# Six of eight sequences routed inside attention, experts begun on part of their tokens

## What is computed

```python
h = layernorm(x) * (1 + ca) + sa
x = x + ga * attention(h)          # layer 0: causal, 16 heads of 16, one shared K and V head, rotary
h = layernorm(x) * (1 + cb) + sb
x = x + gb * experts(h)            # layer 0
# experts: logits = h @ Wg + bg; probs = softmax over the 512 tokens of a sequence, per expert
#          vals, idx = top_k(probs, 64) for each of 8 sequences x 16 experts
#          tok = h[idx]; three 256x256 layers (relu, relu, none); times vals; added back at idx
# layer 1: the same frame, linear attention, then a coupling network of three cycles
```

## Time and profile before

| | us |
|---|---|
| median of 3 runs | 1191.42 (1188.3 to 1193.76) |
| the profiled execution | 1191.18 |
| its span in the trace | 1189.4 |
| PE busy | 1070.3 (90%) |
| DVE, ACT, POOL busy | 733.1, 596.0, 465.7 |
| last logits evicted by ACT | 478.17 |
| tables of the routing done | 503.21 |
| first gather issued, last scatter issued | 507.23, 712.21 |
| first PE work of the linear attention | 722.03 |

### The profile page before, as it was taken

One profiled execution on the slowest core, in us unless ns is written; L12 is line 12 of the kernel. 1 busy time (PEld: TensorE's weight loads), 2 busy tenths in 40 slices (PEclk: granted clock), 3 DMA queues, 4 the chain that ended last, 5 costly groups with the idle time before them and its releaser, 6 DMA issues. The chain is left out here.

```text
span 1189.4 us, 19798 instructions
## 1 busy us (share of the span) xinstructions
PE 1070.3 (90%) x6630; PEld 603.6 (51%) x6630; DVE 733.1 (62%) x1549; ACT 596.0 (50%) x1133; POOL 465.7 (39%) x692
## 2 busy tenths in 40 slices
PE   5499999999999998479999865999999998999996
PEld 3244554454454543346656432556666674455554
DVE  2667878787787783624333323767777781665665
ACT  3167677676766666013333324534444435866732
POOL 2444635444453511068888873333333310000000
PEclk9599999999999999579999987999999998999988
DMA  3522415233241411436676771011211002001001
GB/s 133 112 46 29 82 29 99 63 70 77 57 93 32 73 39 59 150 107 137 165 158 137 178 136 32 6 60 41 77 41 41 19 20 89 1 27 56 25 27 45
DMA packets 73685, 85.31 MB, mean 72 GB/s; under 512 B 12577, under 2 KB 67817, under 8 KB 73457
## 3 DMA queue, kind: packets, MB, share of 16 engines
q1 hardware_dynamic: 61296, 67.27, 21.6%
q0 software_dynamic: 12288, 16.79, 8.2%
HBM read 45.58 MB, written 25.47 MB: 60 GB/s over the span
## 5 line engine op out<-in xcount | busy, mean ns | idle before, releaser
L560 DVE TENSOR_REDUCE nmax<-psum 128x1 f32<-128x512 f32 (+3 forms) x352 | 215.6, 637 | 44.9 <-PE psum L779 39.7
L677 ACT ACTIVATE pT<-psum 128x512 f32<-128x512 f32 x320 | 181.1, 596 | 65.6 <-PE psum L800 35.6
L777 PE MATMUL psum<-k6T,q6T 96*128 96x512 bf16 (+3 forms) x512 | 128.2, 310 | 17.8 <-DVE nmax L560 14.0
L797 PE MATMUL psum<-q6T,k6T 99*128 99x512 bf16 x320 | 119.4, 382 | 1.1 <-ACT pT L677 0.9
L1085 POOL DMA_INDIRECT residual<-expert_y,idx_e x64 | 101.0, 1578 | 22.0 <-issue 16.5
L777 PEld LDWEIGHTS psum<-k6T,q6T 96*128 96x128 bf16 x512 | 45.7, 99 | 91.6 <-DVE nmax L560 59.1
L1604 DVE TENSOR_TENSOR l_scores<-psum,const_sb 128x512 f32<-128x512 f32 x128 | 79.5, 684 | 20.3 <-PE psum L1779 20.3
L779 PE MATMUL psum<-negs_bf,ident_bf 128*128 128x128 bf16 (+2 forms) x352 | 88.8, 252 | 0.0
L812 PE MATMUL psum<-pT,v 128*32 128x512 f32 x640 | 85.0, 604 | 0.0
L1072 POOL DMA_INDIRECT expert_tokens<-router_input,idx_e x64 | 62.7, 980 | 52.4 <-POOLq L903 33.2
L1737 PE MATMUL psum<-l_hT,l_w 128*128 128x512 f32 x128 | 63.7, 621 | 0.8 <-ACT l_plus_one L1681 0.8
(11 more groups left out here) (298 smaller groups left out, 2220.5 us busy)
## 6 DMA issues: line engine op xcount, KB each, us to landing
q6T<-q_parts SPq DMA_DIRECT2D x96, 128.0 KB, 4.5
expert_w<-in_ew SPq DMA_DIRECT2D x16, 768.0 KB, 4.8
x_in<-in_x SPq DMA_DIRECT2D x8, 512.0 KB, 4.3
residual<-x SPq DMA_DIRECT2D x32, 128.0 KB, 1.9
router_input<-h SPq DMA_DIRECT2D x32, 128.0 KB, 1.8
l_x<-residual SPq DMA_DIRECT2D x8, 512.0 KB, 4.3
x_dram<-l_x SPq DMA_DIRECT2D x32, 128.0 KB, 1.7
out<-c_out SPq DMA_DIRECT2D x16, 256.0 KB, 2.1
```

Source lines behind the costliest of these rows:

```text
L560: dve.tensor_reduce(nmax[:, i, u * nh:(u + 1) * nh], ps_s[:, n % SR, 0:nh * (i + 1) * P].rearrange("p (h k) -> p h k", h=nh), AX_X, ALU.ma ...
L677: act.activation(pT[:, n % PR].rearrange("p h t -> p (h t)"), ps_t[:, n % TR, :], ACT.Exp, scale=HD ** -0.5).then_inc(probs, 1)
L777: pe.matmul(out[:, a, :], q6T[0:6 * HD, b % 2, u * nh + a, i * P:(i + 1) * P], k6T[0:6 * HD, b % 2, 0:w], start=a == 0, stop=False, skip_g ...
L797: last = pe.matmul(out, k6T[:, b % 2, j * P:(j + 1) * P], q6T[:, b % 2, hg * 4:hg * 4 + 4, i * P:(i + 1) * P], start=True, stop=j < i)
```

## The change

1. The first sequence's `kv` and `sp` are placed ahead of its second `Q`; only `load_rows(0)` stands before the input of sequence 1, the other two follow the second `qd`; `qd` waits for each part by itself.
2. Logits go straight to SBUF. `lg` of sequence 4 and `h2T` and `lg` of sequence 5 stand earlier in the list (places 910 to 972; they stood at 949, 975, 986, 1007, 1026, 1055). From place 1022 on, every second place is a routing step of sequences 0 to 5 (96 rows): 24 for the rounds, one for the tables (`ti`), one for their transposes (`tt`). Place 1022 follows `("S", 7, 3, 14)`; `tt` stands after `("ST", 7, 3, 0, 1)`.
3. With `lg` of sequence 2, SP loads weights of experts 0 and 1, the second modulation matrix and the biases.
4. The routing block is gone. In the expert block experts 0 to 3 run on tiles 0 to 2, then on tile 3, then the rest on four tiles: 20 units. DVE routes sequences 6 and 7 (32 rows) meanwhile, and ACT evicts both halves in the first four units. PE does the second modulation first. Weights have four slots, in the same memory that later holds buffers of the other phases.

```diff
+EARLY_LOGITS = (910, 925, 937, 950, 962, 972)
+EARLY_ROUTING = (1022, 2)
...
+    for first, later in ((("kv", 0), ("Q", 0, 1)), (("sp", 0, 0), ("kv", 0))):
+        order.remove(first)
+        order.insert(order.index(later), first)
+    b = EARLY_SEQS - 1
+    for at, s in zip(EARLY_LOGITS, [("lg", b - 1)] + [("h2T", b, i) for i in range(NT)] + [("lg", b)]):
+        order.remove(s)
+        order.insert(at, s)
+    for n, s in enumerate([("tk", r, part) for r in range(TOPK // 8) for part in range(3)] + [("ti", 0), ("tt", 0)]):
+        order.insert(EARLY_ROUTING[0] + EARLY_ROUTING[1] * n, s)
...
-                        for b in range(3):
-                            load_rows(b)
+                        load_rows(0)
...
-                        sp.wait_ge(q_lo, 2 * b + half + 1)
                         for place, part in enumerate((0, 0, 0, 1, 1, 2)):
+                            sp.wait_ge((q_hi, q_mid, q_lo)[part], 2 * b + half + 1)
...
+                        if b == 0 and half == 1:
+                            for later in range(1, 3):
+                                load_rows(later)
...
+                    if s == ("lg", 2):
+                        sp.wait_ge(row_fill, 1)
+                        for e in range(2):
+                            sp.dma_start(route.w[:, e].rearrange("p l k c -> p (l k c)"), m.d["ew"][e]).then_inc(route.w_in[e], 16)
+                        sp.dma_start(wmod_l1, m.d["wmod"][:, 1]).then_inc(route.mod_loaded, 16)
+                        sp.dma_start(route.par_e[:, :, 4:7], m.d["eb"]).then_inc(bias_loaded, 16)
...
+                    if s[0] == "tt":
+                        n = EARLY_SEQS * E
+                        pe.wait_ge(tables_ready, 1)
+                        pe.transpose(py[:, 0:n], route.idxf[early_rows].rearrange("p r s -> p (r s)"), ident[0:n, 0:n])
+                        pe.transpose(py[:, P:P + n], route.vals[early_rows].rearrange("p r s -> p (r s)"), ident[0:n, 0:n]).then_inc(y_fill, 1)
...
+UNITS = [(e, (0, 1, 2)) for e in range(EARLY)] + [(e, (3,)) for e in range(EARLY)] + [(e, (0, 1, 2, 3)) for e in range(EARLY, E)]
...
+                first, second, every = (0, 1, 2), (3,), (0, 1, 2, 3)
+                for e in range(EARLY):
+                    gather(e, first)
+                scatter(0, first)
+                scatter(1, first)
+                pool.wait_ge(listed, 1)
+                settle(pool, m.passed)
+                for e in range(EARLY):
+                    gather(e, second)
+                scatter(2, first)
+                gather(EARLY, every)
+                scatter(3, first)
+                for e in range(EARLY):
+                    scatter(e, second)
+                    if e:
+                        gather(e + EARLY, every)
...
+                for r in range(TOPK // 8):
+                    route_round(dve, link, route, late, r, top_ready)
...
+                    if r == 4:
+                        dve.wait_ge(gb_loaded, 16 * B)
+                        gate_outputs(0)
+                gate_outputs(1)
+                dve.wait_ge(exp_ready, 2)
+                route_tables(dve, link, m, late).then_inc(tables, 1)
+                dve.wait_ge(turned, 1)
...
+                gate_outputs(2)
+                copy_tokens(EARLY)
+                gate_outputs(3)
```

More of the change, by code:

```diff
@@ new lines, in route_round @@
+def route_round(dve, link, route, rows, r, top_ready, parts=range(3)):
+    part = slice(8 * r, 8 * r + 8)
+    src = route.left if r else route.logits
+    if 0 in parts:
+        found = dve.max(out=route.top[rows, part], in_=src[rows])
+        if r == TOPK // 8 - 1:
+            found.then_inc(top_ready, 1)
+            dve.wait_ge(top_ready, 1)
+        else:
+            link(found)
+    if 1 in parts:
+        link(dve.max_index(out=route.idx[rows, part], in_max=route.top[rows, part], in_values=src[rows]))
+    if 2 in parts and r < TOPK // 8 - 1:
+        link(dve.match_replace(out=route.left[rows], in_to_replace=route.top[rows, part], in_values=src[rows], imm_value=LOWEST))
@@ new lines, in route_tables, with expert_tables @@
+def route_tables(dve, link, m, rows):
+    route, n = m.route, rows.stop - rows.start
+    seq = m.const[rows, C_SEQ:C_SEQ + 1]
+    link(dve.reciprocal(route.total[rows], route.total[rows]))
+    link(dve.tensor_scalar(route.idxf[rows], route.idx[rows].unsqueeze(1).to_broadcast([n, 2, TOPK]), seq, None, ALU.add))
+    return dve.tensor_scalar(route.vals[rows], route.etop[rows].unsqueeze(1).to_broadcast([n, 2, TOPK]), route.total[rows, 0:1], None,
+                             ALU.mult)
+def expert_tables():
+    number, before, count = {}, [], 0
+    for e, tiles in UNITS:
+        before.append(count)
+        for i in tiles:
+            count += 1
+            number[e, i] = count
+    return number, before
@@ L873, in routing_phase, with expert_phase @@
+def expert_phase(nc, m):
+    TOK, YS, WS = 4, 2, 4
+    number, before = expert_tables()
     with ExitStack() as ctx:
@@ L1038, in expert_phase, with columns @@
         ident = m.const[:, C_IDENT:C_IDENT + P]
+        lead = m.lin
         def par(e, n):
-            return m.par_e[:, e, n:n + 1]
+            return par_e[:, e, n:n + 1]
+        def columns(tiles):
+            return slice(tiles[0] * P, (tiles[-1] + 1) * P)
         with nc.Block() as block:
@@ L1118, in _, with turn @@
             def _(pe):
-                def turn(e, k, tiles=range(4)):
-                    if k == 0 and tiles[0] == 0 and e:
-                        pe.wait_ge(t_act, e)
-                    if k == 1 and e:
-                        pe.wait_ge(t_dve, e)
-                    for i in tiles:
+                def turn(u, k, part):
+                    for i in part:
+                        e, tiles = UNITS[u]
+                        if i == tiles[0] and u:
+                            pe.wait_ge(t_half[k], u)
                         if k == 0:
@@ new lines, in _ @@
+                for u in range(len(UNITS)):
+                    e, tiles = UNITS[u]
+                    at = columns(tiles)
+                    for k in range(KC if u < EARLY else 1):
+                        act.wait_ge(l1_fill, KC * u + k + 1)
+                        if u:
+                            act.wait_ge(l2_fill, KC * u)
+                        act.activation(h1[:, k, at], ps_1[:, k, at], ACT.Relu, bias=par(e, 4)).then_inc(l1_half[k], 1)
+                    if u == 2:
+                        act.wait_ge(top_ready, 1)
+                        act.activation(route.etop[late], route.top[late], ACT.Exp, bias=route.nmax[late, 0:1]).then_inc(exp_ready, 1)
+                    for k in range(KC if u < EARLY else 1):
+                        act.wait_ge(l2_fill, KC * u + k + 1)
+                        if u:
+                            act.wait_ge(l3_fill, before[u])
+                        act.activation(h2[:, k, at], ps_2[:, k, at], ACT.Relu, bias=par(e, 5)).then_inc(l2_half[k], 1)
+                    if u + 1 < len(UNITS):
+                        copy_tokens(u + 1)
+                    for i in tiles:
+                        act.wait_ge(l3_fill, max(number[e, j] for j in tiles if j // 2 == i // 2))
```

465 lines of the change are left out of this document (230 added, 235 removed).

## The result

The changed kernel takes 1193.18 us in the median of 12 runs against 1188.70 of the kernel before (12 runs): ratio 1.0034, 95% interval 1.0020 to 1.0047, so about 4.0 us slower (the medians alone differ by 4.5). Two more series gave 1.0036 (1.0024 to 1.0049) and 1.0034 (1.0018 to 1.0051). I had forecast 1190.7 us, 0.7 less than the profiled execution of before, in a range that holds the result; the size is small, but the sign is wrong.

A forecast was written before the change was run, and what follows sets the result against it. PE was taken to bound mid attention, DVE the exposed routing, POOL's gathers and scatters the experts. Terms -5.0 + 13.5 + 2.6 + 0 - 11.8 = -0.7 against 1191.18 gave 1190.5, as median 1190.7 us; range 1181 to 1200.

The forecast's parts named there:

- start of attention: Attention's start: second sequence's input issued and landed earlier, so score reductions resume sooner; -5.0 us, bounds 3 and 7.
- routing inside attention, clock included: Attention's end: PE waits for DVE's routing rounds and tables, 13.5 us, plus 2.6 us for PE's lowered clock.
- change of block, router to S: Between attention and experts: six logit stores on SP instead of eight, next block starts 0.9 us sooner.
- S: Start of the expert block: predicted at 480.75 us plus the delay from attention's start and the routing inside it.
- S to the end of POOL: Expert phase: from block start to POOL's last scatter, predicted 219.7 us; a change of -10.9 us.
- part 1: Start of attention: fewer row loads ahead of the second sequence's input, reductions resume earlier; gain 5.0 us, bounds 3 and 7.
- Part 4: Expert start: earlier block start and experts on three tiles first, POOL ending the phase; -11.8 us, bounds -6 and -15.
- Part 2: Attention's end: routing six sequences on DVE delays PE 13.5 us (bounds 9 and 15), clock adds 2.6 (0 and 5).
- Part 3: Mid attention: 3.1 MB of loads on SP ahead of the row of maxima stay hidden; 0 us, bounds 0 and 13.
- rival B: Mid attention: the 3.1 MB hold up the row of maxima, below 263 GB/s; 1203.7 us at 124 GB/s; chance 0.12.
- rival C: Expert phase: three-tile units stay near 11.2 us, lists come 8.4 us later, gain only 3.4; 1199 us; chance 0.10.
- Rival A: Attention's end: DVE's routing hides better than counted, half of 16.1 us gone; 1182.6 us; chance 0.25.

The follow-up runs named there:

- the best version: Changed kernel with routing steps three places apart, late lists one unit earlier, modulation matmuls split between attention's end and expert start: 1178.38 us, 0.9907 of the kernel before.

## Why the prediction was wrong

Up to POOL's end the sum can be checked term by term (predicted, and measured from the places in the first table):

| term | predicted | measured |
|---|---|---|
| start of attention | -5.0 | -2.07 |
| routing inside attention, clock included | +16.1 | +16.39 |
| change of block, router to S | -0.9 | +0.44 |
| S to the end of POOL | -10.9 | -8.98 |
| sum | -0.7 | +5.78 |

**The step that failed is part 1**, "Gain 5.0, bounds 3 and 7": 2.07, below its own lower bound, and with 2.9 us the largest row of the 6.5. Part 4 with its change of block missed by 3.3 us inside its bounds; each of the two alone turns the forecast's sign. Three things were in part 1. I took the input's issue at 39.4 us, counting only the row loads; the same diff reorders `kv` and `sp`, which puts three of DVE's gate steps beside GpSimd's wide ones (2.8 us longer together) and lets them begin only 1.4 us earlier, so it was 40.85. I had used the reordering only in its favour; undone by itself it gives about 1 us. The landing took 6.7 us and not 4.5 to 6. And of the 2.6 us that the reductions resume earlier, 2.07 arrive at the outputs. The load mattered as I said: it still holds DVE for 2.98 us.

**Part 2 was right in sum, less so inside.** DVE starts the rounds at 442.33 and ends the tables at 464.58 (I said 465.6 without part 1). In pieces: the lead shrinks step by step where the six steps were moved to, by 1.77 us up to 434.57 (2.07 to 0.30), where I had at most 0.6; the wait adds 12.70 (I took 13.5); the half clock behind it 1.67 (2.6); the last steps 0.25. The 96 rows take the time of 128 (0.69 and 0.68 us a step), which settles that bound. The clock fell as the earlier trace rows suggested, in pieces, and was 0.50 for the six us behind the last wait.

**Part 3 was right**: the 3.1 MB cost nothing, and rival B is out; the lead of 2.07 us is the same 85 us later. But my reason was the wrong one. The time for them doesn't count from the logits, as I took it, but from 11.5 us earlier, where the list reaches the loads. The modulation matrix, issued at 299.86, landed 12.0 us later, at 311.9: 3.1 MB in 13.1 us or 240 GB/s, less than the 263 GB/s under which I let rival B begin. The row of maxima was issued at 314.81, when all had landed. So no run tests what I weighed, the row of maxima behind the weights. But another small load stood right behind them in the same queue, the biases, issued at 300.34:

```profile
par_e<-in_eb SPq DMA_DIRECT2D x1, 24.0 KB, 12.0
```

It landed 12.0 us after its issue, at 312.3, just behind the matrix, where the same load took 3.5 us in the kernel before. The Trainium skill, "DMA: Bandwidth & Descriptors", section "Queues, rings and completion order", says that each DMA engine takes the descriptors of a ring in order; this row agrees. Whether the row of maxima, issued in that time, would have been late was not tested.

**Part 4 was 3.3 us too good.** The lists came at S + 42.0, as worked out, and so did the units (8.5 us from the first scatter group to the second; 8.4 predicted), so rival C is out. The 2.6 us for the first unit's half clock were more than their rows gave (5.88 - 3.60 = 2.3, for four tiles); its first layer took 4.62 us where the next took 2.74. But the block change wasn't shortened: SyncE's six stores into SBUF last 3.73 us, the eight into DRAM lasted 3.68, and 5.43 us lie between the last router matmuls and S where 4.99 did: 1.3 us. And POOL needed 221.6 and not 219.7: expert 1's scatter of tile 3 starts 2.7 us after its own turn and not 1.9, the rest is in the means of its operations, 984 and 1590 ns where the earlier trace rows has 980 and 1578:

```profile
L1117 POOL DMA_INDIRECT residual<-expert_y,idx_e x64 | 101.8, 1590 | 32.7 <-issue 15.5
...
L1104 POOL DMA_INDIRECT expert_tokens<-router_input,idx_e x64 | 63.0, 984 | 32.5 <-issue 26.3
```

**Rival A** fell: the delay was not smaller than worked out. What I hadn't thought of is that the placement was the loose parameter: the same rounds one place further apart cost 11 us less, since I read DVE's idle time only up to 453 us, where the change put the rounds, and not up to 480, where it would have found room. In the sum this stood as a cost correctly worked out; I never asked whether it could be had for much less. With the wider places alone the change would stand near 1.0034 - 0.0090 = 0.994 on a chip without the late finish (an estimate from runs on two chips; on the chip with it, 0.9992 was measured).

One thing stays open. POOL ends 5.8 us later in the first pair of traces, and the runs say 4.0 to 4.3. What follows POOL's end lasts 479.0 us in the trace of before, 473.1 to 476.6 in the changed kernel's three, and 471.8 to 476.6 in all thirteen traces of it and its variants; in two stretches there the granted clock differs (before, then after):

```profile
960.00:1020.00 60.00, 55.54 (x427) 32.56 (x426) 25.53 (x63) 26.47 (x57) 3.41 (x5) 0.91 0.16 54
1140.00:1180.00 40.00, 32.87 (x135) 18.41 (x134) 25.81 (x50) 14.21 (x25) 0.00 (x0) 0.83 0.08 26
```

```profile
960.00:1020.00 60.00, 55.55 (x484) 34.08 (x483) 27.13 (x66) 27.55 (x59) 4.69 (x6) 0.97 0.17 54
1140.00:1180.00 40.00, 33.37 (x152) 18.96 (x151) 27.58 (x54) 14.49 (x25) 0.00 (x0) 0.91 0.08 27
```

With one trace of before, of an execution 2.5 us above its median, it can't be said whether this is its execution or a small gain of the later phases.

## What to carry to other kernels

Work moved under another stage costs what its neighbours wait for, not what it lasts: read the idle time of the engine that gets it over the whole rest of the stage, and spread it as thin as its due date allows before judging the move. Where a change shortens one queue and reorders the steps that feed it, price both on the instruction that is last before the gain. And before taking matmuls off a path, see when the data behind them lands.

## What the runs showed of the hardware

- At the expert start, where TensorE had stood idle before, the modulation's 44 matmuls ran their 10.5 us at a granted clock of 0.50 throughout. Put amid attention's dense work with the routing spread, they took 5.6 us. On one chip their results came 3.1 to 8.2 us behind the modelled end, in four of four traces, with nothing in the records of TensorE to show it. It is seen only on those who wait: two engines that go on at the same instant, long after the releaser's end.
- VectorE instructions over 8x256 f32 took 0.28 to 0.50 us, but 1.23 to 1.37 us beside a GpSimd instruction over 128x512 f32 of 1.15 to 1.44 us (after: 32.61, 34.33, 36.36 us).
- The maximum of eight over 512 columns takes 0.68 to 0.69 us for 96 and for 32 rows as for 128: the rounds for two sequences cost DVE as much as those for eight. (32 rows, from the changed kernel's expert start:)

```profile
496.45 0.69 DVE L973 MAX8 route_top<-router_logits 32x8 f32<-32x512 f32 x1 [7.80 <-PEq L313]
```

- With PE busy 15.3 of 25 us the mean granted clock was 0.85, and 0.50 in the six us of dense work behind the last wait; in the best version, with PE busy 22.2 of the same 25 us, it was 1.00.
